# Cross-attention on one core: scores of all sixteen heads in four row groups and four banks, with one maximum and one subtraction per tile

## The reference, cut to what matters

```
q = split_heads(x @ Wq.T + bq)          # 32 tiles, 16 heads of 8 features, 128 rows
k, v = split_heads(ctx @ Wk.T + bk), split_heads(ctx @ Wv.T + bv)     # 77 context rows
attn = softmax(einsum('bhqd,bhkd->bhqk', q, k) / sqrt(8), axis=-1)
x = x + einsum('bhqk,bhkd->bhqd', attn, v) @ Wo.T + bo      # with layer norms around it
```

## Time and profile before

| | us |
|---|---|
| median of 3 runs (701.08 to 702.3) | 701.19 |
| the profiled execution's own time | 698.5 |
| its span, first to last instruction | 696.5 |
| the loop over 32 tiles, first maximum to end of the last subtraction | 13.9 to 215.3 |

### The profile page before, as it was taken

The page is one execution under the profiler, slowest core; times in us unless marked ns, Lnnn a source line. Parts: engine busy times, 40 slices in busy tenths (PEclk is TensorE's granted clock), DMA queues, the critical chain, the costliest instruction groups (busy, mean ns, idle before and its releaser), DMA issues. The chain is left out here.

```text
span 696.5 us, 15660 instructions
## 1 busy us (share of the span) xinstructions
PE 645.4 (93%) x5160; PEld 487.2 (70%) x5160; DVE 451.8 (65%) x1336; ACT 338.1 (49%) x738; POOL 382.6 (55%) x502
## 2 busy tenths in 40 slices
PE   7999999999999689999998999999999899999990
PEld 4566666666667568999997546555554699999990
DVE  3676788788787857886779877877554233324433
ACT  3444454454443344444666756776543445444440
POOL 5312265765755854655677676667555244555552
PEclk9999999999999889999999999999999999999996
DMA  6831112112110168888883300000102888888975
GB/s 183 235 71 11 9 20 31 35 20 29 36 28 20 55 185 246 249 265 258 261 251 103 106 29 31 28 24 31 32 23 65 267 270 267 274 252 281 277 219 169
DMA packets 102118, 91.34 MB, mean 131 GB/s; under 512 B 52952, under 2 KB 85848, under 8 KB 101720
## 3 DMA queue, kind: packets, MB, share of 16 engines
q1 hardware_dynamic: 88679, 70.25, 36.1%
q0 software_dynamic: 8640, 17.84, 7.3%
q10 hardware_dynamic: 4721, 2.27, 1.2%
HBM read 69.14 MB, written 22.72 MB: 132 GB/s over the span
## 5 line engine op out<-in xcount | busy, mean ns | idle before, releaser
L701 POOL DMA_INDIRECT y_tok<-ysb,xr x142 | 138.6, 976 | 117.1 <-DVE ysb L1149 56.5
L625 POOL DMA_INDIRECT xs_sorted<-xa,slot_i x128 | 130.6, 1020 | 79.9 <-DVE slot_i L1055 44.1
L1544 PE MATMUL pair<-xT,w_all 128*128 128x256 f32 (+1 forms) x640 | 138.0, 360 | 0.0
L1544 PEld LDWEIGHTS pair<-xT,w_all 128*128 128x128 f32 x640 | 108.5, 194 | 9.5
L1878 PEld LDWEIGHTS pair<-w_all,hT 128*128 128x128 f32 x852 | 106.4, 192 | 5.6 <-issue 1.7
L1878 PE MATMUL pair<-w_all,hT 128*128 128x128 f32 x852 | 108.2, 276 | 1.9 <-DVE xT L1127 1.0
L878 ACT ACTIVATE hT<-pair,w_all 128x256 f32<-128x256 f32 (+1 forms) x160 | 62.5, 447 | 72.9 <-PE pair L1544 72.1
L1127 DVE COPY xT<-pair 128x256 f32<-128x256 f32 (+1 forms) x80 | 31.4, 393 | 90.0 <-PE pair L1547 86.4
L941 ACT ACTIVATE hS<-pair,w_sh 128x512 f32<-128x512 f32 x64 | 44.0, 687 | 54.9 <-PE pair L1544 54.1
L1544 PE MATMUL pair<-xeT_all,w_sh 128*128 128x512 f32 x128 | 67.6, 611 | 0.0
L1941 PE MATMUL pair<-hS,w_sh 128*128 128x512 f32 x128 | 65.6, 595 | 0.0
(11 more groups left out here) (222 smaller groups left out, 1081.3 us busy)
## 6 DMA issues: line engine op xcount, KB each, us to landing
w_all<-in_w SPq DMA_DIRECT2D x40, 578.0 KB
w_all<-in_w SPq DMA_DIRECT2D x40, 450.0 KB
xa<-y_tok SPq DMA_DIRECT2D x32, 256.0 KB, 4.4
xr<-xs_sorted SPq DMA_DIRECT2D x62, 130.0 KB
y_tok<-ysb,xr POOLq DMA_INDIRECT x142
xs_sorted<-xa,slot_i POOLq DMA_INDIRECT x128, 2.3
xs_sorted<-in_pads SPq DMA_DIRECT2D x12, 130.0 KB, 4.2
xs_sorted<-in_pads SPq DMA_DIRECT2D x18, 65.0 KB, 3.8
```

The source lines that it names most:

```text
L625: g.indirect_dma_start(xs_dram[l], bass.IndirectOffsetOnAxis(ap=slot_i[:, i:i + 1], axis=0), xa[:, GT * c + j // TOPK, j % TOPK, :], None)\
L701: g.indirect_dma_start(y_dram[l], bass.IndirectOffsetOnAxis(ap=xr[u % NXR][:, t, P:P + 1].bitcast(I32), axis=0), ysb[u % NYB][:, t, :], None)\
L1544: return mm(out_, l_, r_, start=True, stop=True)
```

## The change

Banks 0 to 3 now take the scores of all sixteen heads, one row group and bank for each four heads, issued at once; `score_max` and `score_sub` are one instruction each over 1232 columns, and `sm` is one tile of 1232 columns and padding, not two halves. The turns go to banks 4 and 5. `summed` and `weighted` write the second half of bank 5 (`weighted_at`), for the tile at hand, at the end of its loop turn. `weighted_kept` (ACT) copies both out after every tile, and `add_sums` (DVE) adds up the four tiles' sums, which PE did before. `expand` moves to the end of step 1 on PE, `output` to DVE's first window of step 2 (between the maximum and the subtraction), and it reads the expanded inverses from the bank, so ACT's copy of them goes. `logits` and both rounds of `choose` move to the second window, `keep_input` and `norm_input` on ACT behind the exponentials.

```diff
+        weighted_at = bank[5][:, 2 * P:4 * P].rearrange("p (b c) -> p b c", b=2)
...
# ACT
-                        after(act, S("pvd_done"), T - 1)
                         after(act, S("pvn_done"), T - 1)
...
+                def weighted_kept(T):
+                    u, t = divmod(T, GT)
+                    act.wait_ge(S("pvn_done"), T + 1)
+                    if t == 0:
+                        after(act, S("o_ready0"), u - 1)
+                    copy_out(nd[:, u % 2:u % 2 + 2, t * P:(t + 1) * P], weighted_at).then_inc(S("nd_kept"), 1)
...
                     if live(v):
                         exps(T, (2, 3))
+                    if s == 0 and live(v - 2):
+                        keep_input(v - 2)
+                    if s == 1 and live(v + 1):
+                        norm_input(0, v + 1, xn0)
+                    if live(v):
+                        weighted_kept(T)
...
# DVE
+                def score_sub(T):
+                    after(dve, S("t_done"), NG * T)
+                    v.tensor_tensor(sm[:, 0:2 * SPAN].rearrange("q (b h k) -> q b h k", b=NG, k=NK), scores,
+                                    maxima.unsqueeze(3).to_broadcast([P, NG, HG, NK]), ALU.subtract).then_inc(S("s_sub"), 1)
...
+                def add_sums(u, t):
+                    dve.wait_ge(S("nd_kept"), GT * u + t + 1)
+                    before = nd[:, 1, 0:P] if t == 1 else rden[:]
+                    link(v.tensor_tensor(rden[:], before, nd[:, 1, t * P:(t + 1) * P], ALU.add))
...
                 def output(u):
-                    dve.wait_ge(S("rdx_ready"), u + 1)
-                    dve.wait_ge(S("pvn_done"), GT * (u + 1))
-                    v.tensor_tensor(oT0, bank[4][:], rdx[:], ALU.mult).then_inc(S("o_ready0"), 1)
+                    dve.wait_ge(S("rdx_done"), u + 1)
+                    v.tensor_tensor(oT0, nd[:, u % 2 * 2, :], bank[rdx_bank(u)][:], ALU.mult).then_inc(S("o_ready0"), 1)
...
                 def first_window(v_, s):
-                    if s == 1 and live(v_ - 2):
-                        logits(v_ - 2)
-                    if s == 2 and live(v_ - 2):
-                        choose(0, v_ - 2, 0)
+                    if s == 2 and live(v_ - 1):
+                        output(v_ - 1)
                     if s == 3 and live(v_ - 1):
                         residual(v_ - 1)
...
                     if live(v_):
-                        score_max(T, 0)
-                        score_sub(T, 0)
+                        score_max(T)
                     first_window(v_, s)
                     if live(v_):
-                        score_max(T, 1)
-                        score_sub(T, 1)
+                        score_sub(T)
                     second_window(v_, s)
# PE
+                    after(pe, S("s_sub"), T)
+                    for gr in range(NG):
+                        r = slice(32 * gr, 32 * gr + 32)
+                        last = one(bank[gr][:, 0:HG * NK], tile(qT4[u % 2], t)[r, :], kblk[u % 2][t][r, :])
...
-                    if live(v):
-                        score(T, 1)
+                    if 0 <= T + 1 < NT:
+                        score(T + 1)
...
-                    if T > 0 and s <= 1:
-                        weighted(T - 1)
-                    if T > 0 and s > 0:
-                        summed(T - 1)
...
+                    if live(v):
+                        summed(T)
+                        weighted(T)
+                    if s == 0 and live(v - 2):
+                        kept_turned(v - 2)
+                    if s == 1 and live(v - 1):
+                        expand(v - 1)
```

More of the change, by code:

```diff
@@ L287, in build @@
         wide = [sb(f"wide{g}", [P, 512]) for g in range(NG)]
-        smax = [sb(f"smax{i}", [P, 2 * HG]) for i in range(2)]
-        sm = [sb(f"sm{i}", [P, NCK * P]) for i in range(2)]
+        smax = sb("smax", [P, H])
+        sm = sb("sm", [P, SPAN + NCK * P])
         kf4 = sb("kf4", [P, GT * NK])
         rden = sb("rden", [P, P])
-        rdx = sb("rdx", [P, GT * P])
+        nd = sb("nd", [P, 3, GT * P])
         cxm = sb("cxm", [P, 3, GT * H])
@@ L369, in build @@
         table = sb("table", [1, 1])
-        pairs = [ctx.enter_context(nc.psum_tensor(f"pair{i}", [P, 1024], F32)) for i in range(4)]
+        quads = [ctx.enter_context(nc.psum_tensor(f"quad{i}", [P, 2048], F32)) for i in range(2)]
+        pairs = [q[:, i * 1024:(i + 1) * 1024] for q in quads for i in range(2)]
         bank = [p[:, i * 512:(i + 1) * 512] for p in pairs for i in range(2)]
@@ L835, in attention0 @@
                         exps(T, (0, 1))
[L836 to L841, removed]
                     if s == 2 and live(v + 1):
@@ L1315, in second_window @@
                         inverse_sums(v_ - 1)
[L1316 to L1321, removed]
                     if s == 3 and live(v_ - 1):
@@ L1326, in second_window @@
                         moments(0, 0, "ln", v_ + 2)
+                    if s == 1 and live(v_ - 2):
+                        logits(v_ - 2)
+                    if s == 2 and live(v_ - 2):
+                        choose(0, v_ - 2, 0)
+                        choose(0, v_ - 2, 1)
+                    if s == 3 and live(v_ - 2):
+                        sums(0, v_ - 2)
+                    if s > 1 and live(v_):
+                        add_sums(v_, s - 1)
                 def key_bias():
@@ L1630, in busy, with score @@
                         one(bank[b][:, 0:reps * P], warm[:], warm[:].unsqueeze(1).to_broadcast([P, reps, P]))
-                def score(T, ab):
+                def score(T):
                     u, t = divmod(T, GT)
-                    if t == 0 and ab == 0:
+                    if t == 0:
                         pe.wait_ge(S("qT_ready"), u + 1)
                         pe.wait_ge(S("kblk_ready"), u + 1)
[L1637 to L1640, removed]
+                    after(pe, S("s_sub"), T)
+                    for gr in range(NG):
+                        r = slice(32 * gr, 32 * gr + 32)
+                        last = one(bank[gr][:, 0:HG * NK], tile(qT4[u % 2], t)[r, :], kblk[u % 2][t][r, :])
                     last.then_inc(S("s_done"), 1)
@@ L1645, in turns @@
                         G = NG * T + gr
-                        pe.wait_ge(S("s_sub"), 2 * T + gr // 2 + 1)
+                        pe.wait_ge(S("s_sub"), T + 1)
                         after(pe, S("exp_done"), G - 1)
+                        if gr == 1:
+                            after(pe, S("nd_kept"), T)
                         for i in range(unit_columns(gr) // P):
-                            last = turn(tile(bank[2 + gr % 2], i), tile(sm[gr // 2], 3 * (gr % 2) + i))
+                            last = turn(tile(bank[4 + gr % 2], i), tile(sm[:, gr // 2 * SPAN:], 3 * (gr % 2) + i))
                         last.then_inc(S("t_done"), 1)
@@ L1668, in weighted @@
                             at = (gr * 3 + i) * 32
-                            last = mm(tile(bank[4], t)[r, :], vm(u, t)[:, at:at + 32], weights_of(T, gr, i),
+                            last = mm(weighted_at[r, u % 2, :], vm(u, t)[:, at:at + 32], weights_of(T, gr, i),
                                       start=(i == 0), stop=(i == 2))
@@ L1683, in summed @@
                             at = (t * 6 + gr % 2 * 3 + i) * 32
-                            last = mm(bank[5][r, 0:P], dcst[:, at:at + 32], weights_of(T, gr, i),
-                                      start=(t == 0 and i == 0), stop=(t == GT - 1 and i == 2))
-                    last.then_inc(S("pvd_done"), 1)
+                            mm(weighted_at[r, 1 - u % 2, :], dcst[:, at:at + 32], weights_of(T, gr, i), start=(i == 0), stop=(i == 2))
                 def logits(u):
@@ L1755, in attention0 @@
                         busy(1, 2)
-                    if live(v):
-                        score(T, 1)
-                    if s == 1 and live(v - 2):
-                        logits(v - 2)
+                    if 0 <= T + 1 < NT:
+                        score(T + 1)
                     if live(v):
@@ L1763, in attention0 @@
                         busy(1, 4, 6)
-                    if s == 1 and live(v - 1):
-                        expand(v - 1)
+                    if s == 1 and live(v - 2):
+                        logits(v - 2)
                     if s == 2 and live(v + 1):
@@ L1770, in attention0 @@
                         column_sums(0, v - 2)
-                    if T > 0 and s > 1:
-                        weighted(T - 1)
-                    if T > 0 and s == 0:
-                        summed(T - 1)
-                    if 0 <= T + 1 < NT:
-                        score(T + 1, 0)
                     if live(v):
```

49 lines of the change are left out of this document (15 added, 34 removed).

## The result

The changed kernel takes 720.72 us (median of 4 runs, 718.42 to 725.06) against 701.30 us beside it: 1.0288 times the time before, with a 95% interval of 1.0252 to 1.0324. Forecast were 719 us, in a range of 704 to 734.

What follows compares the result with a forecast made beforehand. The prediction took a ring that PE and DVE turn together as the bound. Loop 218.5 against 201.4 (+17.1) and +1.1 behind it gave 701.2 + 18 = 719 us, range 704 to 734.

Steps and rivals of the forecast that it cites:

- Row groups: Scores of all heads on PE: four row groups share their time, 0.08 us more, turns load at 0.80.
- The rival in which they do not share their time: Scores on PE, about 20 steps: 0.7 us more wherever PE is the bound, 733 us; chance 0.08.
- Maximum and subtraction: On DVE, one instruction each over 1232 columns: 1.45 us, 32 of each.
- steps 0 to 3: The four loop turns of a full group: 6.05, 8.9, 7.1 and 6.0 us, sum 28.05 against 26.4 before.
- step 1: Loop turn with logits, values and expand on PE, then output and subtraction on DVE before the next scores: 8.9 us.
- the hold of 2.3: Step 1: PE has nothing for 2.3 us, since scores need the subtraction behind output, which needs expand.
- step 2: Loop turn with choose, add_sums, maximum, residual and subtraction on DVE: 7.1 us, DVE the bound, PE ready at about 6.
- The rival of the ring that wins: Loop: half the PE-to-DVE hand-overs gone, steps are PE's own, a group 24 us; 692 us in all; chance 0.09.
- The values: Group 1's values land at 49.2; with group 0 at 22.5 us, tile 4's numerators wait 4.9 us on PE.
- The clock: PE's clock falling after the wait for values at tile 4: 1 us taken, range 0 to 4.
- The rival said that it falls in every group: PE's holes halve the clock for 3.4 us in seven groups: 719 + 14 = 733 us; chance 0.10.
- Behind the loop: From the last subtraction to the end of the last output: 7.85 us, +1.1 against before.

Runs made afterwards that it cites:

- the second experiment: Changed kernel with the output product on VectorE behind the subtraction of step 2 instead of ahead of it: 708.9 us, ratio 1.0111 to the kernel before.
- the first experiment: Changed kernel with expand ahead of the sums and numerators in step 1 instead of behind them: 701.25 us, ratio 0.9987 to the kernel before.
- the first one with fillers: Changed kernel with short matmuls whose results nobody reads issued on TensorE where it stood still: 718.3 us, ratio 1.0229 to the kernel before.
- the third experiment: Changed kernel with the load of group 1's values issued ahead of the loop that writes the pads: 717.6 us, ratio 1.0249 to the kernel before.
- the kernel with both edits and fillers: Changed kernel with expand ahead of sums, group 1's values loaded ahead of the pads, and unread short matmuls in the loop: 691.43 us, ratio 0.9837.

## Why the prediction was right

**Row groups: right, and a little less than taken.** The load of four groups' scores to the load of the turns took 0.73 (130.37 to 131.10, in the rows of the steps) against 0.72; I took 0.08 more. The Trainium skill ("TensorE: Matmul & The Clock Gate", Part 3) has 3.07 times the throughput for four row tiles. By the forecast's estimate from that figure it would have been 0.1 to 0.2 more; the trace shows 0.01. The rival in which they do not share their time is out.

**Maximum and subtraction: right.** 1.45 by two widths, 1.43 and 1.44 measured.

**The steps: right, each a little long.** Forecast for steps 0 to 3 6.05, 8.9, 7.1, 6.0; measured 5.86, 8.50, 6.97, 5.96. The sum, 28.05, is 0.75 too long, half of that in step 1. That the hold of 2.3 is one chain (expand, output, subtraction, scores) is shown by the first two experiments: the hold goes with either order. For step 2 the forecast had PE ready at about 6 and VectorE as the bound. The trace has two chains of nearly one length: the subtraction ends 6.74 us after the step's first load, and the queries' copy, which ACT makes behind its copy of the numerators, 6.92 after it. So the length was right, and the second chain was put 0.9 too short. The second experiment shows that VectorE has no room there: it took the 0.69 us put into it at full price. The rival of the ring that wins needed the wait of step 1 not to hold PE, with a group of 24 us; the first experiment made that case, and the group was 24.7.

**The values: right in place, short by size.** Forecast were group 0 in 22.5, a wait of 4.9 us, numerators at 49.2. Measured: 25.24, a wait of 3.18, numerators at 50.98. At a clock of 1.00 group 0 takes 23.2, so 0.7 of the miss is my count of steps and 2.0 the clock, 0.91 here, which I had put nowhere in group 0. The values came 1.8 later because SP's issues moved from 37.07 to 38.76; I had held them to be fixed. The numerators follow that issue by 12.2 to 12.4 us in the changed kernel, in the two with one edit of PE's or VectorE's order, and in the first one with fillers, while the issue itself lies between 37.75 and 39.28. A slower group 0 and a shorter wait offset each other, as the fillers showed from the other side.

**The clock: the step that was mis-sized, twice.** The rival said that it falls in every group, for 14 us. It did fall in every group of the middle, and cost 0.1 to 0.2 us in each, since the stretch lies in step 3, where PE waits for VectorE anyway: the third experiment's groups 3 to 6, with the same hold and a clock of 1.00, take 27.14 to 27.42. In the forecast I had 1 us for the wait of tile 4 and nothing for group 0, which lost 2.0. Behind the wait the clock was at half for 6.8 us (51.6 to 58.4), and from the numerators to the end of group 1 the trace has 19.8 us. At a clock of 1.00, and without the hold, that is 14.5 (45.08 to 59.62 in the kernel with both edits and fillers); less the hold's 2.4 some 2.8 are left for the clock, by subtraction. Together that is near 5 us where the sum had 1.

**Behind the loop: short.** From the last subtraction's end to the end of the last `output` I put 7.85. The rows (timeline):

```profile
231.79 1.44 DVE L1275 TENSOR_TENSOR sm<-quad,smax 128x1232 f32<-128x1232 f32 x1
...
235.88 1.51 PE L1688 MATMUL quad<-hS,xeT_all 128*32 128x128 f32 x24 [0.33 <-ACT hS L781]
237.16 1.51 PE L1675 MATMUL quad<-hS,w_all 128*32 128x128 f32 x24
...
241.82 0.68 DVE L1298 TENSOR_TENSOR lent<-nd,quad 128x512 f32<-128x512 f32 x1
```

It is 9.3 (233.23 to 242.50), 1.4 more: sums and numerators ran at 1.2 GHz, 1.51 each against 0.86 (217.29 in the timeline of before) and 0.84. The last subtraction ended at 233.23; forecast was near 232. By the end of that `output` the kernel is 20.4 behind (242.50 against 222.09), and 19.8 at the end of the span.

So the total came out through errors of both signs: groups 3 to 6 together 3.0 too long, group 7 0.5; groups 0 to 2 together 4.4 too short, the end 1.4. That they nearly cancel is luck. What carried the forecast is the hold, which is shown: without it the time is that of the kernel before. That the rest, values, end and clock, just eats the 0.7 to 1.5 us a group that the change does win without the hold (25.7 to 26.4 before, 24.7 to 25.0 in the first experiment, groups 2 to 6) is a sum of rows, and not one experiment.

## What to carry to other kernels

When two halves of a buffer that were freed one by one become one that is freed at once, list for each engine what stands between reading that buffer and freeing it. One instruction there that waits for another engine turns a saving into a hold, and moving it by some lines gives the saving back. A fall of the clock is worth what the engine's step is worth: 0.1 to 0.2 us where another engine bounded it, 1.5 us where it lasted longer and reached into step 0, whose end waits for PE's own work (the second experiment's group 4); so remove the waits first and fill holes afterwards. A transfer that lands just in time before an edit that makes its reader earlier is the next wait.

## What the runs showed of the hardware that was not expected

Four row groups of 308 columns cost 0.73 us to the next load where two cost 0.72. In the changed kernel PE's granted clock fell to half once in each group of the middle, behind steps 1 and 2, in which PE waited 2.4 and 1.35 us. The waits alone do not decide it: in the third experiment groups 3 to 6 kept 1.00 with a wait of 2.39 in step 1 and of 1.38 and 1.19 in steps 2 and 3 of group 3, and in the first experiment, with the hold gone, they kept it too, with 1.35 and 1.19. What decides it stays open. And group 0, whose own instructions on PE are the same in all of them, had a clock of 1.00 in both kernels with short matmuls in its holes, and without them 1.00 in two and 0.86 to 0.93 in four, the changed one's 0.91 among these.
